# Attention kernel: the first output chunk moved between the values and the scores, and the sum of tops put in front of the values

## What is computed

```
q = split_heads(x @ Wq.T);  k = split_heads(ctx @ Wk.T);  v = split_heads(ctx @ Wv.T)
probs = softmax(q k^T / sqrt(32))
out = merge_heads(probs @ v) @ Wo.T + bo + x
```

## Time and profile before

| | |
|---|---|
| median of 3 runs | 425.37 us (425.2 to 425.66) |
| the profiled execution | 425.4 us |
| span of its trace | 423.6 us |
| PE busy | 415.6 us, 98% of the span |
| ACT, POOL, DVE busy | 304.4, 305.1, 264.0 us |
| granted TensorE clock | 1.00 in the whole span, the 2.4 GHz level |

### The profile page before, as it was taken

One profiled execution on the slowest core, in us unless ns is written; L12 is line 12 of the kernel. 1 busy time (PEld: TensorE's weight loads), 2 busy tenths in 40 slices (PEclk: granted clock), 3 DMA queues, 4 the chain that ended last, 5 costly groups with the idle time before them and its releaser, 6 DMA issues.

```text
span 423.6 us, 8284 instructions
## 1 busy us (share of the span) xinstructions
PE 415.6 (98%) x2552; PEld 230.5 (54%) x2552; DVE 264.0 (62%) x546; ACT 304.4 (72%) x590; POOL 305.1 (72%) x267
## 2 busy tenths in 40 slices
PE   8999999999999999999999999999999999999996
PEld 6877775677776644444444444444444444444442
DVE  0355676766678777756677656765677655556723
ACT  1637888857678898999667975888667966966720
POOL 8326799999679597988649594769649594764560
PEclk9999999999999999999999999999999999999999
DMA  7998636555965465334753446334744446345203
GB/s 270 365 326 268 236 110 210 171 180 160 310 206 195 156 207 199 128 136 161 251 177 127 136 152 238 126 139 175 251 160 132 145 155 218 136 168 191 82 26 124
DMA packets 41781, 77.33 MB, mean 183 GB/s; under 512 B 5264, under 2 KB 6416, under 8 KB 41744
## 3 DMA queue, kind: packets, MB, share of 16 engines
q1 hardware_dynamic: 30944, 57.21, 38.9%
q10 hardware_dynamic: 10800, 19.67, 14.3%
HBM read 33.40 MB, written 10.49 MB: 104 GB/s over the span
## 4 chain that ended last, share of the span: by engine, by line
PE 87%; ACT 3%; POOL 3%; DMA 3%; SPq 2%; issue 1%; DVE 1%; ACTq 0%; DVEq 0%; POOLq 0%
PE ps_q L939 28%; PE ps_o L939 27%; PE ps_s L1006 10%; PE ps_pv L1013 7%; PE ps_m L990 6%; PE ps_den L1018 4%; PE ps_o L910 2%; DMA x_f<-in_x 2%; POOL p_lo L456 2%; PE ps_m L1063 1%; DMA q_packed<-mxT 1%; SPq L374 1%; PE ps_q L1063 1%; POOL x_lo L447 1%; PE ps_o L1063 1%
## 5 line engine op out<-in xcount | busy, mean ns | idle before, releaser
L456 POOL TENSOR_TENSOR p_lo<-p_f,p_hi 77x512 f16<-77x512 f32 x160 | 182.9, 1165 | 84.5 <-ACT p_hi L592 83.5
L939 PE MATMUL ps_o<-attn,wo 128*128 128x512 f16 x435 | 109.0, 381 | 0.2
L588 ACT ACTIVATE p_f<-ps_s 77x512 f32<-77x512 f32 x160 | 94.3, 589 | 20.3 <-PE ps_s L1006 19.2
L726 DVE TENSOR_REDUCE mx<-ps_m 128x4 fp32r<-128x308 f32 x160 | 69.2, 475 | 42.0 <-PE ps_m L990 40.7
L592 ACT ACTIVATE p_hi<-ps_s 77x512 f16<-77x512 f32 x160 | 93.6, 585 | 2.4 <-PE ps_den L1018 2.3
L939 PE MATMUL ps_q<-x,wq 128*128 128x512 f16 x375 | 85.0, 379 | 0.0
L1006 PE MATMUL ps_s<-q_packed,k_packed 128*77 128x512 f32 x160 | 64.4, 445 | 0.2
L939 PEld LDWEIGHTS ps_o<-attn,wo 128*128 128x128 f16 x435 | 35.6, 98 | 46.7 <-issue 13.1
L939 PEld LDWEIGHTS ps_q<-x,wq 128*128 128x128 f16 x375 | 36.6, 98 | 44.5 <-issue 0.5
L715 DVE SCALAR_TENSOR_TENSOR q_lo<-ps_q,q_scale,q_hi 128x512 fp32r<-128x512 f32 x25 | 18.8, 751 | 50.3 <-ACT q_hi L571 50.3
L990 PE MATMUL ps_m<-k_diag,q_hi 128*128 128x308 f32 x160 | 43.4, 351 | 0.7 <-ACT q_hi L571 0.7
(11 more groups left out here) (127 smaller groups left out, 599.2 us busy)
## 6 DMA issues: line engine op xcount, KB each, us to landing
q_packed<-q_hi SPq DMA_DIRECT2D x80, 256.0 KB, 2.5
x_f<-in_x SPq DMA_DIRECT2D x45, 256.0 KB, 4.1
q_packed<-q_lo SPq DMA_DIRECT2D x40, 256.0 KB, 3.3
x_res<-in_x ACTq DMA_DIRECT2D x35, 256.0 KB, 2.7
out<-x_res ACTq DMA_DIRECT2D x35, 256.0 KB, 2.7
wq_sb<-in_wq SPq DMA_DIRECT2D x10, 320.0 KB, 4.6
wo_sb<-in_wo SPq DMA_DIRECT2D x10, 320.0 KB, 4.0
wk_sb<-in_wk SPq DMA_DIRECT2D x8, 320.0 KB, 5.8
```

The source lines that it names most:

```text
L456: nc.gpsimd.tensor_tensor(p_lo[:, i, :], p_f[:, i, :], p_hi[:, i, :], ALU.subtract).then_inc(plo_done, 1)
L588: nc.scalar.activation(p_f[:, i, :], ps_s[i % 2][0:L, :], ACT.Exp, scale=SCALE).then_inc(pf_done, 1)
L726: nc.vector.tensor_reduce(mx[:, g % RS, :, tt], ps_m[tt % 2][:, 0:HG * L].rearrange("p (h k) -> p h k", k=L), AX_X, ALU.max).then_inc(max_ ...
L939: last = nc.tensor.matmul(ps[:, :], w[:, k, P * c:P * (c + 1)], a[:, c, :], start=(c == 0 and n == 0), stop=(c == G - 1 and n == 2))
```

## The change

For an output tile in fp16 halves and from step 17 (3, 2) on, `behind` is true: chunk 0 of the output projection is issued directly behind `values`, and what were chunks (0, 1), (2, 3), (4) at the three later places is now (1, 2), (3, 4) and none. Steps 17 to 39 are 23 steps. In (4, 1), (5, 1) and (6, 1), where ps_o must first be given up by the sum, `sum_tops` moves in front of `values` and the wait for `sums_read` in front of chunk 0. The programs of DVE, ACT, POOL and SP stay as they are.

```
+                sum_first = has_sums(t, g) and (not isinstance(t, int) or t >= 4)
+                if sum_first:
+                    sum_tops(t, g)
                 values(last_t, last_g, batch(last_t))
+                behind = bool(tiles) and o_in_half(tiles[0][0]) and (sum_first or not has_sums(t, g))
+                if sum_first:
+                    pe.wait_ge(sums_read, sums_so_far(t, g))
+                if behind:
+                    project_out(*tiles[0], (0,))
                 if exists(t):
                     scores(t, g, 0, batch(t))
                     scores(t, g, 1, batch(t))
-                if has_sums(t, g):
+                if has_sums(t, g) and not sum_first:
                     sum_tops(t, g)
...
-                if has_sums(t, g):
+                if has_sums(t, g) and not sum_first:
                     pe.wait_ge(sums_read, sums_so_far(t, g))
                 if tiles:
-                    project_out(*tiles[0], (0, 1))
+                    project_out(*tiles[0], (1, 2) if behind else (0, 1))
...
                 if tiles:
-                    project_out(*tiles[0], (2, 3))
+                    project_out(*tiles[0], (3, 4) if behind else (2, 3))
...
-                if tiles:
+                if tiles and not behind:
                     project_out(*tiles[0], (4,))
```

## The result

| | before | changed |
|---|---|---|
| median, us | 425.51 (11 runs, 425.06 to 426.46) | 426.53 (11 runs, 426.24 to 427.33) |
| ratio | 1 | 1.0026, 95% interval 1.0017 to 1.0036 |
| span of the trace, us | 423.6 | 424.6 |

The change makes the kernel slower by about 1.0 us; the ratio is 1.0026. The forecast was 427.3, slower by 1.9 us. All comparisons here are between runs at a granted clock of 1.00 (0.998 at the least).

The account below looks back on a forecast made before the run. PE, busy 98% of the span, was taken as the bound. Terms -0.90 + 2.72 + 0.59 - 0.65 + 0.10 = +1.86 us on the profiled 425.4 gave 427.3 us; the main case's own range was 426.4 to 428.3.

Parts of the forecast that it names:

- main case: Whole kernel: forecast 427.3 us, own range 426.4 to 428.3, chance 0.70.
- 15 plain steps: Steps without special waits: the edge from values to scores gets cheaper, gain 0.06 us each, -0.90 us together.
- extra in (7, 1): PE's chunk 4 in step (7, 1) waits for POOL's low halves of attn: +0.1 us.
- three pairs with a sum: Steps (t, 0) and (t, 1) of tiles 4 to 6: PE waits at the sum for DVE's tops, +2.72 us (2.1 to 3.3).
- last step: Ahead of last_tiles(0): PE waits for helpers' rows made late by the scores, +0.59 us (between 0 and 0.65).
- step (3, 2): Moved matmuls fill the 0.72 us wait of max_scores for q_hi: -0.65 us.
- third rival: No measurable change: DVE's and ACT's lateness is swallowed in part, sum steps cost 2.1, 426.0 us; chance 0.12.
- 0.59 us later: In a changed step, first scores, maxima and the helpers' work waiting for them come 1.21 - 0.62 = 0.59 us later.
- d: Sum steps: delay from the tops' end to the values, taken as 0.5 us, with 0.3 and 0.7 as bounds.
- the next lock: Sum steps: were the tops no obstacle, PE would wait for the sums' read instead, some 0.9 us.
- slower by more: Second rival: sum steps make ACT late too, some five places lose 0.3 to 0.5 more, 429.3 us; chance 0.12.

Follow-up runs that it names:

- e2: Changed kernel with only the first of the chunk's three matmuls behind the values, the other two at the head of the first output piece; 425.65 us, one run.
- e4: Changed kernel with the chunk in front of the values instead of behind them, and the sum steps in the order of before; 426.58 us, one run.
- e10: Kernel before with row maxima 0 and 1 in front of scores 0 and 1 in steps from 17 on without a sum, no chunk moved; 426.74 us, one run.
- e7: Changed kernel with only DVE's program altered: two of the three tops of steps (t, 0), t at least 4, found earlier; 425.42 us, one run.
- e8: Changed kernel with two tops found early and DVE also reading the sums in front of q_lo instead of behind it; 422.92 us, one run.
- e5: Changed kernel with the sum steps and the last step (7, 4) back in the order of before; 423.86 us, ratio 0.9964 to the kernel before.
- e6: Kernel before with the chunk behind the values in step (3, 2) alone; 424.59 us, one run.

## Why the prediction was right, point by point

**In whole.** The direction and the mechanism were right, the size was nearly twice too large: +1.9 us forecast, +1.0 measured. 426.53 lies in the main case's own range (426.4 to 428.3) only just. The terms, in us, with the measured step lengths beside them:

| term | forecast | measured |
|---|---|---|
| 15 plain steps, (7, 1) among them | -0.90 | -0.86 |
| extra in (7, 1) | +0.10 | none |
| three pairs with a sum | +2.72 | +2.09 |
| last step | +0.59 | +0.60 |
| step (3, 2) | -0.65 | -0.65 |
| sum | +1.86 | +1.18 |

The sum steps came out at the 2.1 that the third rival took, which ends at 426.0; what keeps the result above it is the last step, whose wait came in full.

**What bounds.** Right: PE throughout, with single waits.

**Plain steps.** Right in reason, and nearly in size. Fourteen steps gained 0.71 us together, 0.03 to 0.08 each and 0.05 in the mean, where 0.06 was counted. The fifteenth, (7, 3), gained 0.15, and 0.12 of it not at the edge: its scores of head 2 took 0.35 in the chain of the kernel before and 0.23 in the changed one. In the kernel before they start at 390.81, 0.06 after ACT's p_hi of head 0 ends at 390.75, so a short wait for ACT is likely there; that is argued, not shown. So it is in part luck that the fifteen come to 0.86. e2 shows that one fp16 matmul is enough, e4 that the chunk brings nothing elsewhere, e10 that the loss grows with the first weight load.

**0.59 us later.** Right where the helpers wait for PE: the tops ended 10.24 us after the values of (5, 0) instead of 9.63.

**Sum steps.** The mechanism was right and the size too high: 2.09 us where 2.72 was predicted. The step that was off is d, from the end of the tops to the values. It was counted as 0.24 + 0.19 + 0.10 = 0.5, and measured as 0.26 in all three places (274.03 to 274.29 in (5, 1)): 0.05 to the weight load, 0.19 for that load, 0.02 to the values. That is below the 0.3 that I gave as its lower end. The 0.24 was taken from the chunk's wait for the read in (5, 1), inside the loop, where register rows stand ahead of the chunk. The same wait in (4, 1), outside the loop, shows 0.06 in the kernel before (228.14 + 0.17 to 228.37), so its trace already had the smaller value:

```profile
228.14 0.17 DVE L801 TENSOR_SCALAR sums<-ps_o 128x10 f32<-128x10 f32 x1 [0.20 <-PE ps_o L932]
228.37 1.47 PE L939 MATMUL ps_o<-attn,wo 128*128 128x512 f16 x6
```

The 0.10 for the edge into the values was counted twice: a step length runs from the start of the values to the next such start, and the first two rounds take 0.55 in the chain at the sum as in every plain step, so what that edge costs was already in the 9.35. Three times 0.24 is 0.72 us, the whole gap of the sum of terms (1.18 against 1.86) and a little more. I also named the next lock, the read behind q_lo, with some 0.9 us; e7 shows it at about 0.6 to 0.8, its steps (t, 1) of 10.05 to 10.22 against 9.37 to 9.43 in e8.

**The last step.** Right: +0.60 against +0.59, and e5 takes it back.

**Step (3, 2).** Right: -0.65, and alone in e6.

**Step (7, 1).** Wrong, and small: +0.1 was predicted, and the step has no wait. POOL's low halves of attn start at 368.27 in the changed kernel:

```profile
368.27 5.63 POOL L463 TENSOR_TENSOR attn<-attn 128x512 f16<-128x512 f32 x5
```

Set against the values of (7, 0) at 359.62 that is 8.65 us, before 367.17 - 358.91 = 8.26: 0.39 later, not 0.59. In (7, 0) of the kernel before, ACT began its exponentials without waiting for PE, as its row without an idle time shows:

```profile
360.83 0.58 ACT L588 ACTIVATE p_f<-ps_s 77x512 f32<-77x512 f32 x1
```

In the changed kernel the same row waits for PE:

```profile
361.90 0.59 ACT L588 ACTIVATE p_f<-ps_s 77x512 f32<-77x512 f32 x1 [0.27 <-PE ps_s L1006]
```

It starts 2.28 us after the values instead of 1.92, so 0.36 later and not 0.59: ACT was late by its own work before, and part of the shift was swallowed there.

**Rivals.** Of "slower by more", ACT's lateness came as worked out and stayed harmless. q_hi of (5, 1) starts 284.70 - 283.65 = 1.05 us after the values:

```profile
284.70 0.66 ACT L571 ACTIVATE q_hi<-ps_q,q_scale 128x512 fp32r<-128x512 f32 x1
```

The prediction cites the Trainium skill, page TensorEngine Tiling, Key Properties: changing the tiling mode drains the TensorE. The page gives no figure. The 0.10 us that pass in all three kernels before the first weight load starts agree with a cost that is paid whatever stands behind the values; the rest of the loss, 0.06 us for the scores and 0.10 for the maxima, changes with the weights, which that rule does not cover. No run separates the two further.

## What to carry to other kernels

When a matmul group is moved on a full TensorE, price the edge it leaves and the one it makes, and then count how much later everything on the other engines becomes; look for the few places where one of these is due within that time. Those places, not the many plain steps, decided the sign here, and each could be given its own order: the plain and the waiting step take the gain, the sum and the last step keep the old order, or the tops and the read move too. A step that is moved ahead of other work can have a second wait right behind the first; here e7 removed one and found the other. When the price of a wait is taken from a row, take it from the same kind of place: the 0.24 of the loop was four times the 0.06 outside it.

## What the runs showed of the hardware

Behind the four side-by-side 32-column matmuls, the first weight load of the next group starts some 0.10 us later than a next round would have, in all three kernels, and the loss in all equals the length of that load: 0.10, 0.16 and 0.20 us for loads of 98, 146 and 188 ns. Whether it is the whole load, or a fixed 0.10 and the rest of the load, stays open.

From the end of DVE's last top to the start of PE's weight load that waited for it passed 0.05 us. From the end of the sums' read to the chunk passed 0.06 us in the steps outside the loop and 0.24 us in (5, 1) and (6, 1), inside it, in the kernel before. The sum itself also stands in the loop there, but with no register row right ahead of it, and in the changed kernel it started with the short delay. Both contrasts speak for the register rows as the cause; no run took them out.
